# Maxima over the partitions by transposes on TensorE and maxima on VectorE in place of GpSimd's all-reduce, with the opening order of all engines written anew

## The chip, the cores and the metric

The kernel runs on one core of one Trainium2 chip, as one launch. The metric is the device time of an execution in microseconds. In the text PE is TensorE, DVE is VectorE, ACT is ScalarE, GpSimd is also POOL, and SP is SyncE, which here issues all the DMAs.

## The reference

A block of cross-attention and a feed-forward network with quantised weights and activations, over x of 8 x 1024 x 512 and a context of 8 x 64 x 384, all float32:

1. x is normalised (mean and variance over the 512, no weights) and gives q = norm(x) Wq. The context gives k = ctx Wk and v = ctx Wv. There are 8 heads of 64. Softmax of q k / 8 times v, times Wo, plus bo, is added to x.
2. The sum is normalised again and goes through three "bit-linear" layers: silu(norm(x) times w_gate) times (norm(x) times w_up), then w_down (512 x 2048 each), and the result is added to x. Each of these weights is divided by the mean of its absolute values, rounded and clipped to -1, 0, 1. Each row of activations is scaled by 127 over its largest absolute value and rounded.

## The kernel before, in words

**Tiles and stages.** x is cut into 64 tiles of 128 rows, 8 tiles to each of the 8 batches. Attention runs six tiles ahead of the feed-forward part (L = 6). Per tile: stats and rstd (mean, variance and 1/sqrt; the last on GpSimd), x_norm (DVE), x_hi and x_lo (the tile as two float16 halves; ACT and GpSimd), turn_x (a DMA transpose), scores (PE), s_max, expo, e_sum, p_norm, p_hi and p_lo (softmax, and again two halves), turn_p, attend, add_x. Then stats, x_scale, quant_x, copy_x, turn_q (quantise and transpose), gate_up (PE), silu (ACT), mult and h_part (DVE), h_max, quant_h, copy_h, turn_h, down (PE), final and store_y.

**Keys and values are folded into the weights.** For each batch scores multiply by Wq times K (round_X 0 to 3, lines 1067 to 1071) and attend by V times Wo (round_X 4 to 7). K and V lie on block diagonals (block_diag, line 813). All these operands are two float16 halves (hi on ACT, lo on DVE), and so that the halves are exact enough each operand is first scaled by a power of two taken from its largest absolute value.

**The maxima.** Four such values are needed over a whole operand, all partitions included: of Wq (m = 0) and Wo (m = 1), one number each, and of K and V, eight numbers each, one per batch. DVE takes the maximum along each partition (max_w, line 752; max_c, line 758) into mxw; then GpSimd's partition_all_reduce takes it over the partitions and leaves the result on all of them in mxa (lines 532 to 538):

```python
def all_max_w(m):
    eng.wait_ge(v_mw, m + 1)
    eng.partition_all_reduce(mxa[:, m, 0:1], mxw[:, m, 0:1], P, RABS).then_inc(g_mw, 1)
```

scale_w, scale_c and scales (lines 767 to 797) make the powers of two from mxa. What needs them: q_hi, q_lo and o_wide (Wq and Wo in halves), block_diag, and hi and lo.

**The opening.** Setup 0 to 2 transpose the context, setup 3 to 6 make K, 7 to 10 transpose Wq, 11 to 14 make V (line 1025). The three weights of the feed-forward part, 4 MB each, are loaded in four pieces; abs_sum (ACT and DVE) sums their absolute values, total (PE) adds over the partitions, mean (DVE, line 836) gives the scale. Then the pieces are made ternary: 24 quarters through a PE transpose (flip), ACT (tern_flip, line 650) and DVE (clip_flip), the rest through tern, clip and a DMA transpose (turn_w). load_down overwrites gate's pieces and waits for them (line 482). The first gate_up needs all of gate and up.

**What sets the order.** Every engine executes its pieces in the order written and waits by semaphores. Each piece has a due time (put), and the pieces are sorted by it; but those named in the engine's list in OPENING (line 331) come first, in the order of the list. The lists of before reach to about the first tile of the feed-forward part (down 0 on PE). SP's list holds the loads and the DMA transposes, so a turn_x that waits holds back the loads behind it.

## Time and profile before

| what | us |
|---|---|
| median of 3 runs | 1204.06 |
| lowest and highest run | 1202.31, 1204.07 |
| span of the profiled execution | 1203.5 |
| busy in it: PE | 1102.5 |
| busy: DVE | 1091.2 |
| busy: ACT | 701.0 |
| busy: POOL | 429.4 |

The profiled execution has no other time of its own than its span, from the first to the last instruction; the median of the runs is 0.56 us above it. An engine's line in the page shows its busy share in 40 slices of 30 us, in tenths. "Idle before" an instruction is put down to what it waited for last ("<-"); "issue" is idle time for which the trace shows no event.

### The profile page before, as it was taken

The page shows a single profiled execution, that of the slowest core. Times are in us where ns is not written, and L with a number is a line of the kernel's source. Part 1 is how long each engine was busy: PE and PEld are TensorE (multiplying, and loading weights), DVE is VectorE, ACT ScalarE, POOL GpSimd, SP SyncE. Part 2 cuts the span into 40 slices and gives each one's busy share as a digit, 9 for nine tenths or more (in the row PEclk, how much of TensorE's full clock was granted, in tenths as well). Part 3 has the DMA queues.
Part 4 walks back from the last instruction along what each step waited for, and adds up shares of the span by engine and source line. Part 5 has one row for each costly group of instructions (what it writes and reads, how often), then busy time and mean ns, then how long its engine had stood idle before and what let it go on. Part 6 is the DMA issues. An engine that isn't in the chain of part 4 may idle for free.

```text
span 1203.5 us, 17256 instructions
## 1 busy us (share of the span) xinstructions
PE 1102.5 (92%) x5204; PEld 509.8 (42%) x5266; DVE 1091.2 (91%) x2463; ACT 701.0 (58%) x883; POOL 429.4 (36%) x534
## 2 busy tenths in 40 slices
PE   5636889999999999999999999999999999999998
PEld 3323434444444444444444444444444444444433
DVE  4449999999999999999999999999999999999996
ACT  2336676656665665666656665656556665565544
POOL 1037623434343343334333433333333344334100
PEclk9768999999999999999999999999999999999999
DMA  7724585454453454544544555345545455444343
GB/s 279 218 71 114 120 157 101 101 93 99 108 112 85 103 105 110 97 88 105 109 96 93 103 110 106 89 94 110 107 88 104 101 114 105 97 106 81 79 92 92
DMA packets 343484, 130.65 MB, mean 109 GB/s; under 512 B 319968, under 2 KB 320480, under 8 KB 342880
## 3 DMA queue, kind: packets, MB, share of 16 engines
q1 hardware_dynamic: 343392, 129.55, 48.8%
q8 instruction: 42, 0.69, 0.2%
q14 instruction: 50, 0.41, 0.1%
HBM read 34.08 MB, written 16.78 MB: 42 GB/s over the span
## 4 chain that ended last, share of the span: by engine, by line
DVE 48%; PE 27%; issue 15%; DMA 4%; ACT 3%; POOL 1%; DVEq 0%; SPq 0%; ACTq 0%; POOLq 0%
PE ps L1142 13%; DVE FF L882 7%; DVE hm L886 7%; PE ps L1158 5%; DVE bns L868 4%; DVE FF L939 3%; PE ps L1082 3%; PE ps L1083 3%; PE ps L1085 3%; DVE am L940 2%; DVE den L927 2%; DMA FF<-FF 2%; DVE xr L959 2%; DVE xr L874 2%; ACT FF L666 2%
## 5 line engine op out<-in xcount | busy, mean ns | idle before, releaser
L1142 PE MATMUL ps<-wgT,FF 128*128 128x512 bf16 x1024 | 267.7, 384 | 32.3 <-DMA FF<-FF 32.1
L1142 PE MATMUL ps<-wW,FF 128*128 128x512 bf16 x1024 | 267.8, 385 | 0.0
L675 ACT ACTIVATE FF<-FF,c 128x1024 int16<-128x1024 f32 x128 | 140.0, 1141 | 178.6 <-DVE c L896 178.6
L1158 PE MATMUL ps<-wW,FF 128*128 128x512 bf16 x962 | 218.4, 379 | 5.9 <-DMA FF<-FF 2.6
L666 ACT ACTIVATE FF<-ps,sg 128x512 f32<-128x512 f32 x256 | 172.3, 675 | 20.0 <-PE ps L1142 19.2
L886 DVE TENSOR_REDUCE hm<-FF 128x1 f32<-128x512 f32 x256 | 174.2, 680 | 4.6
L882 DVE TENSOR_TENSOR FF<-FF,ps 128x512 f32<-128x512 f32 x256 | 172.3, 673 | 3.1 <-PE ps L1142 2.3
L1142 PEld LDWEIGHTS ps<-wgT,FF 128*128 128x128 bf16 x1024 | 96.5, 98 | 157.9 <-DMA FF<-FF 50.9
L544 POOL TENSOR_SCALAR ve<-mv 128x1 f32<-128x1 f32 x128 | 47.7, 373 | 306.2 <-DVE mv L869 275.5
L1142 PEld LDWEIGHTS ps<-wW,FF 128*128 128x128 bf16 x1024 | 101.2, 99 | 124.9 <-issue 6.6
L1158 PEld LDWEIGHTS ps<-wW,FF 128*128 128x128 bf16 x1024 | 99.9, 98 | 124.3 <-issue 4.5
L564 POOL TENSOR_TENSOR AT<-AT,rd 128x512 f32<-128x512 f32 x64 | 66.9, 1045 | 230.8 <-DVE rd L931 230.8
L682 ACT ACTIVATE xhl<-xn 128x512 f16<-128x512 f32 x64 | 40.3, 629 | 146.7 <-DVE xn L910 145.1
L552 POOL TENSOR_TENSOR xhl<-xn,xhl 128x512 f16<-128x512 f32 x64 | 74.6, 1166 | 109.5 <-ACT xhl L682 102.8
L1082 PE MATMUL ps<-MV,xT 128*128 128x512 f16 x256 | 99.4, 388 | 4.7 <-DVE AT L921 4.2
L1083 PE MATMUL ps<-MV,xT 128*128 128x512 f16 x256 | 99.3, 388 | 0.0
L1082 PE MATMUL ps<-MV,pT 128*128 128x512 f16 x256 | 97.0, 379 | 0.6 <-DVE MV L809 0.6
L1083 PE MATMUL ps<-MV,pT 128*128 128x512 f16 x256 | 97.0, 379 | 0.0
L693 ACT ACTIVATE AT<-AT 128x512 f16<-128x512 f32 x64 | 40.3, 630 | 90.5 <-POOL AT L564 86.5
L572 POOL TENSOR_TENSOR AT<-AT 128x512 f16<-128x512 f32 x64 | 74.1, 1158 | 51.9 <-POOL AT L564 44.5
L546 POOL TENSOR_TENSOR rs<-ve,half 128x1 f32<-128x1 f32 x128 | 84.6, 661 | 10.7
L868 DVE BATCH_NORM_STATS2 bns<-xr 128x6 f32<-128x512 f32 x128 | 86.1, 673 | 0.5 <-DMA xr<-in_x 0.5
(120 smaller groups left out, 1647.3 us busy)
## 6 DMA issues: line engine op xcount, KB each, us to landing
xr<-in_x SPq DMA_DIRECT2D x64, 256.0 KB, 2.8
out<-xr SPq DMA_DIRECT2D x64, 256.0 KB, 2.0
FF<-in_L_ffn_w_gate SPq DMA_DIRECT2D x4, 1024.0 KB, 11.7
wW<-in_L_ffn_w_up SPq DMA_DIRECT2D x4, 1024.0 KB, 8.9
FF<-in_L_ffn_w_down SPq DMA_DIRECT2D x4, 1024.0 KB, 5.3
FF<-FF SPq DMA_TRANSPOSE x192, 3.2
MV<-in_L_xattn_Wq SPq DMA_DIRECT2D x1, 1024.0 KB, 8.2
MV<-in_L_xattn_Wo SPq DMA_DIRECT2D x1, 1024.0 KB, 11.8
```

The costliest lines, as they stand in the source:

```text
L546: eng.tensor_tensor(rs[:, t:t + 1], ve[:, t:t + 1], half[:, :], ALU.pow).then_inc(end, 1)
L552: eng.tensor_tensor(xhl[:, 1, :], xn[:, :], xhl[:, 0, :], ALU.subtract).then_inc(g_xl, 1)
L572: eng.tensor_tensor(phl[:, 1, :], E[:, j % 2, :], phl[:, 0, :], ALU.subtract).then_inc(g_pl, 1)
L666: eng.activation(h[:, i % 2, f * 512:(f + 1) * 512], G[n % 2][:, :], ACT.Silu, scale=sg[:, i:i + 1]).then_inc(a_si, 1)
L675: eng.activation(q16h[:, 1024 * z:1024 * z + 1024], h[:, t % 2, 1024 * z:1024 * z + 1024], ACT.Copy, scale=c2[:, t:t + 1]).then_inc(a_qh, 1)
L868: link(eng.bn_stats(bns[:, k, t % 2, :], xr[:, t % R, :]))
L882: eng.tensor_tensor(hh, hh, U[n % 2][:, :], ALU.mult).then_inc(v_h, 1)
L886: ins = eng.tensor_reduce(hm[:, f:f + 1], h[:, i % 2, f * 512:(f + 1) * 512], AX_X, ALU.max, apply_absolute_value=True)
L1082: eng.matmul(bank[:, :], T[:, k, :], hi[:, k, :], start=(k == 0), stop=False)
L1083: eng.matmul(bank[:, :], T[:, k, :], lo[:, k, :], start=False, stop=False)
L1142: mm = eng.matmul(bank[n % 2][:, :].rearrange("p (o f) -> p o f", o=4), qxT[:, i % 2, k, :], w[:, 4 * f:4 * f + 4, k, :], start=(k == 0), ...
L1158: mm = eng.matmul(y_bank(i)[:, :], hT[:, i % 2, c, :], wdT[:, c, :], start=(c == 0), stop=(c == 15))
```

## The change

The four partition_all_reduce calls and their semaphores go. Each of the four maxima (e = 0 and 1: Wq and K; e = 2 and 3: Wo and V) now takes five steps on PE and DVE: max_turn transposes a 128 x 128 tile whose first columns hold the maxima of the partitions (PE, into a PSUM bank); max_fold takes the maximum along each row of it and copies that over 128 columns (DVE); max_spread transposes this back, so that each partition has all the numbers (PE); max_take copies them into mxa (DVE). The tile mxc is cleared by GpSimd at the start. e = 0 uses the bank of scores, the others that of attend. round_X 0 and 1 and attend 0 get waits for these banks.

The lists of all five engines in OPENING are written anew and are longer: SP's to load_x 14, PE's to gate_up 5 2, DVE's to copy_h 4 1. In SP's list x 0 comes before Wq, gate 3 and the loads of up before turn_x 0, gate 2 after gate 3. In DVE's list stats 1 to 3 and block_diag 1 0 come earlier, before mean 0. The diff, with each list cut to its beginning:

```diff
 def xattn_ffn(nc, x, ctx_768, Wq, Wk, Wv, Wo, bo, w_gate, w_up, w_down, out):
@@ -120,7 +119,9 @@
         wsum = sb("wsum", [P, 3, 4], F32)
         wst = sb("wst", [P, 3, 4], F32)
         mxq = sb("mxq", [P, 2, 4, NB], F32)
-        mxw = sb("mxw", [P, 2, 1 + NB], F32)
+        mxc = sb("mxc", [P, 4, P], F32)
+        mxr = sb("mxr", [P, P], F32)
+        mxf = sb("mxf", [P, 4], F32)
         mxa = sb("mxa", [P, 2, 1 + NB], F32)
         e2 = sb("e2", [P, 2, NB], F32)
         inv = sb("inv", [P, 2, NB], F32)
@@ -162,10 +163,13 @@
         v_mx = sem("v_mx")
         g_ow = sem("g_ow")
         v_mw = sem("v_mw")
-        g_mx = sem("g_mx")
+        g_mc = sem("g_mc")
+        p_mt = sem("p_mt")
+        v_mf = sem("v_mf")
+        p_mb = sem("p_mb")
+        v_mc = sem("v_mc")
         v_ch = sem("v_ch")
         v_sc = sem("v_sc")
-        g_mw = sem("g_mw")
         v_sw = sem("v_sw")
         v_sk = sem("v_sk")
         a_wh = sem("a_wh")
@@ -328,66 +332,93 @@
         def bank_of(n):
             return FIRST_BANKS[n] if n < 8 else pX
 
+
+        def max_bank(e):
+            return pS if e == 0 else pA
+
+        def max_dst(e):
+            m = e // 2
+            return mxa[:, m, 0:1] if e % 2 == 0 else mxa[:, m, 1:1 + NB]
+
             "sync": (
+                "load_ctx, load_wk, load_x 0, load_wq, load_x 2, load_x 3, load_gate 0, load_x 8, load_bo, load_up "
+                "0, load_wv, load_gate 1, load_x 1, load_wo, load_gate 3, load_up 1, load_gate 2, load_up 2, load_x "
+                "7, turn_x 0, load_up 3, load_x 5, load_x 4, load_x 6, turn_x 1, load_down 0, turn_x 2, load_down "
+                "1, turn_x 3, turn_p 0, load_down 2, turn_x 4, turn_p 1, load_down 3, turn_p 2, turn_x 5, turn_p 3, "
...
             "gpsimd": (
+                "constants, rstd 0 0, x_lo 0, add_bo 0, rstd 1 0, rstd 2 0, rstd 3 0, add_bo 1, o_wide 0, o_wide 1, "
+                "o_lo 0, o_lo 1, o_wide 2, o_wide 3, x_lo 1, o_lo 2, o_lo 3, add_bo 2, x_lo 2, add_bo 3, p_norm 0, "
+                "x_lo 3, p_lo 0, rstd 4 0, p_norm 1, add_bo 4, x_lo 4, p_lo 1, rstd 5 0, add_bo 5, rstd 6 0, rstd 7 "
...
             "scalar": (
+                "evac 0, evac 2, x_hi 0, evac 4, evac 5, evac 6, q_hi 0, q_hi 1, q_hi 2, q_hi 3, evac 11, abs_sum 0 "
+                "1, evac 12, evac 13, hi 0 0, hi 0 1, hi 0 2, abs_sum 0 3, abs_sum 1 0, abs_sum 1 1, evac 14, hi 0 "
+                "3, o_hi 0, o_hi 1, x_hi 1, o_hi 2, o_hi 3, abs_sum 1 3, tern_flip 0 0 0, tern_flip 0 0 1, "
+                "tern_flip 0 0 2, tern_flip 0 0 3, x_hi 2, tern_flip 0 1 0, tern_flip 0 1 1, expo 0, tern_flip 0 1 "
...
             "vector": (
+                "evac 1, stats 0 0, x_norm 0, max_w 0, evac 3, max_c 0 0, max_fold 0, max_c 0 1, abs_sum 0 0, "
+                "max_take 0, max_c 0 2, scale_w 0, max_c 0 3, q_lo 0, max_fold 1, q_lo 1, max_take 1, q_lo 2, "
+                "scale_c 0, q_lo 3, block_diag 0 0, scales 0, stats 1 0, stats 2 0, stats 3 0, x_norm 1, max_w 1, "
+                "max_c 1 1, lo 0 0, lo 0 1, lo 0 2, block_diag 1 0, max_fold 2, max_c 1 2, max_take 2, max_c 1 0, "
+                "scale_w 1, abs_sum 0 2, max_c 1 3, mean 0, max_fold 3, abs_sum 1 2, lo 0 3, max_take 3, scale_c 1, "
+                "block_diag 0 1, x_norm 2, clip_flip 0 0 0, clip_flip 0 0 1, s_max 0, clip_flip 0 0 2, clip_flip 0 "
+                "0 3, clip_flip 0 1 0, clip_flip 0 1 1, x_norm 3, scales 1, e_sum 0, clip_flip 0 1 2, s_max 1, "
+                "clip_flip 0 1 3, stats 4 0, clip_flip 0 2 0, e_sum 1, s_max 2, x_norm 4, clip_flip 0 2 1, "
...
             "tensor": (
+                "setup 0, setup 1, setup 2, setup 3, setup 4, max_turn 0, setup 5, max_spread 0, setup 6, setup 7, "
+                "setup 8, setup 9, setup 10, max_turn 1, max_spread 1, setup 11, setup 12, setup 13, round_X 0 0, "
+                "round_X 0 1, round_X 0 2, round_X 0 3, setup 14, max_turn 2, max_spread 2, total 0, max_turn 3, "
+                "max_spread 3, flip 0 0 0, flip 0 0 1, scores 0, total 1, flip 0 0 2, flip 0 0 3, round_X 0 4, flip "
...
         block = ctx.enter_context(nc.Block())
@@ -528,14 +559,7 @@
                 eng.memset(kbd[:, :, :, :], 0.0).then_inc(g_c, 1)
                 eng.memset(vbd[:, :, :, :], 0.0).then_inc(g_c, 1)
                 eng.wait_ge(g_c, 4)
-
-            def all_max_w(m):
-                eng.wait_ge(v_mw, m + 1)
-                eng.partition_all_reduce(mxa[:, m, 0:1], mxw[:, m, 0:1], P, RABS).then_inc(g_mw, 1)
-
-            def all_max(m):
-                eng.wait_ge(v_mx, m + 1)
-                eng.partition_all_reduce(mxa[:, m, 1:1 + NB], mxw[:, m, 1:1 + NB], P, RABS).then_inc(g_mx, 1)
+                eng.memset(mxc[:, :, :], 0.0).then_inc(g_mc, 1)
 
                 mv, ve, rs, done, mid, end = ((mv1, ve1, rs1, v_st1, g_ve1, g_rs1),
@@ -584,10 +608,6 @@
             for c in range(4):
                 put(25.9 + c, o_wide, c)
                 put(26.1 + c, o_lo, c)
-            put(MAXW_T[0] + 2.3, all_max_w, 0)
-            put(MAXW_T[1] + 2.3, all_max_w, 1)
-            put(MAX_T[0], all_max, 0)
-            put(MAX_T[1], all_max, 1)
             for s in range(FIRST, LAST + 1):
                 if 0 <= j + 1 < NT:
@@ -752,7 +772,8 @@
             def max_w(m):
                 eng.wait_ge((l_wq, l_wo)[m], 16)
                 src = (wq_sb, wo_sb)[m]
-                eng.tensor_reduce(mxw[:, m, 0:1], src.rearrange("p c n -> p (c n)"), AX_X, ALU.max,
+                eng.wait_ge(g_mc, 1)
+                eng.tensor_reduce(mxc[:, 2 * m, 0:1], src.rearrange("p c n -> p (c n)"), AX_X, ALU.max,
                                   apply_absolute_value=True).then_inc(v_mw, 1)
 
             def max_c(m, q):
@@ -761,11 +782,23 @@
                                         ALU.max, apply_absolute_value=True)
                 link(ins)
                 if q == 3:
-                    eng.tensor_reduce(mxw[:, m, 1:1 + NB], mxq[:, m, :, :].rearrange("p q b -> p b q"), AX_X,
+                    eng.wait_ge(g_mc, 1)
+                    eng.tensor_reduce(mxc[:, 2 * m + 1, 0:NB], mxq[:, m, :, :].rearrange("p q b -> p b q"), AX_X,
                                       ALU.max).then_inc(v_mx, 1)
 
+            def max_fold(e):
+                eng.wait_ge(p_mt, e + 1)
+                if e >= 1:
+                    eng.wait_ge(p_mb, e)
+                link(eng.tensor_reduce(mxf[:, e:e + 1], max_bank(e)[:, 0:P], AX_X, ALU.max))
+                eng.tensor_copy(mxr[:, :], mxf[:, e:e + 1].to_broadcast([P, P])).then_inc(v_mf, 1)
+
+            def max_take(e):
+                eng.wait_ge(p_mb, e + 1)
+                eng.tensor_copy(max_dst(e), max_bank(e)[:, 0:1 if e % 2 == 0 else NB]).then_inc(v_mc, 1)
+
             def scale_w(m):
-                eng.wait_ge(g_mw, m + 1)
+                eng.wait_ge(v_mc, 2 * m + 1)
                 link(eng.tensor_scalar(we[:, m, 0:1].bitcast(I32), mxa[:, m, 0:1].bitcast(I32), 0x7F800000, None,
                                        ALU.bitwise_and))
                 link(eng.tensor_scalar(we[:, m, 0:1], we[:, m, 0:1], 2.0 ** -45, 2.0 ** 45, ALU.max, ALU.min))
@@ -773,7 +806,7 @@
                 eng.tensor_scalar(wf[:, m:m + 1], we[:, m, 1:2], 2.0 ** 14, None, ALU.mult).then_inc(v_sw, 1)
 
             def scale_c(m):
-                eng.wait_ge(g_mx, m + 1)
+                eng.wait_ge(v_mc, 2 * m + 2)
                 link(eng.tensor_reduce(ke[:, m, 0:1], mxa[:, m, 1:1 + NB], AX_X, ALU.max))
                 link(eng.tensor_scalar(ke[:, m, 1:2].bitcast(I32), ke[:, m, 0:1].bitcast(I32), 0x7F800000, None,
                                        ALU.bitwise_and))
@@ -785,7 +818,7 @@
                 back = (2.0 ** -11, 2.0 ** -23)[m]
                 eng.wait_ge(v_sk, m + 1)
                 eng.wait_ge(v_sw, m + 1)
-                eng.wait_ge(g_mw, m + 1)
+                eng.wait_ge(v_mc, 2 * m + 2)
                 link(eng.tensor_scalar(e2[:, m, :], mxa[:, m, 1:1 + NB], mxa[:, m, 0:1], None, ALU.mult))
                 link(eng.tensor_scalar(e2[:, m, :].bitcast(I32), e2[:, m, :].bitcast(I32), 0x7F800000, None,
                                        ALU.bitwise_and))
@@ -968,6 +1001,9 @@
                 put(MAXW_T[m], max_w, m)
                 for q in range(4):
                     put(SET_E[(3, 11)[m] + q] + .7, max_c, m, q)
+                for e, w in ((2 * m, (MAXW_T[0] + 1, MAX_T[0] + 3)[m]), (2 * m + 1, MAX_T[m])):
+                    put(w + .6, max_fold, e)
+                    put(w + .9, max_take, e)
                 put(MAXW_T[m] + 3.2, scale_w, m)
                 put(MAX_T[m] + 1.2, scale_c, m)
                 put(MAX_T[m] + 1.3, block_diag, 0, m)
@@ -1049,9 +1085,24 @@
                                         start=(a == 0), stop=(a == 2))
                 mm.then_inc(p_set, 1)
 
+            def max_turn(e):
+                eng.wait_ge((v_mw, v_mx)[e % 2], e // 2 + 1)
+                if e == 0:
+                    eng.wait_ge(g_id, 2)
+                elif e >= 2:
+                    eng.wait_ge(v_lo, 2)
+                    eng.wait_ge(v_mc, e)
+                eng.transpose(max_bank(e)[:, 0:P], mxc[:, e, :], ident[:, :]).then_inc(p_mt, 1)
+
+            def max_spread(e):
+                eng.wait_ge(v_mf, e + 1)
+                eng.transpose(max_bank(e)[:, 0:P], mxr[:, :], ident[:, :]).then_inc(p_mb, 1)
+
             def round_X(b, r):
                 n = 8 * b + r
                 bank = bank_of(n)
+                if n < 2:
+                    eng.wait_ge(v_mc, n + 1)
                 if r < 4:
                     eng.wait_ge(v_kb, 4 * b + 4)
                 else:
@@ -1099,6 +1150,8 @@
                 eng.wait_ge(t_p[j % 2], 16 * (j // 2 + 1))
                 if j % TPB == 0:
                     eng.wait_ge(v_lo, 8 * b + 8)
+                if j == 0:
+                    eng.wait_ge(v_mc, 4)
                 if j >= 1:
                     eng.wait_ge(v_x1, j)
                 three(pA, pT[:, j % 2, :, :], part(b, 2), part(b, 3)).then_inc(p_A, 1)
@@ -1160,6 +1213,9 @@
 
             for r in range(SETUP):
                 put(SET_T[r], setup, r)
+            for e, w in enumerate((MAXW_T[0] + 1, MAX_T[0], MAX_T[0] + 3, MAX_T[1])):
+                put(w + .5, max_turn, e)
+                put(w + .8, max_spread, e)
             for r in range(8):
                 put(RND_T[r], round_X, 0, r)
             for m in range(3):
```

## Rows read from the trace of the kernel before

**Rows 1.** The page, section 1, and the slices of DVE in section 2.
```profile
PE 1102.5 (92%) x5204; PEld 509.8 (42%) x5266; DVE 1091.2 (91%) x2463; ACT 701.0 (58%) x883; POOL 429.4 (36%) x534
...
DVE  4449999999999999999999999999999999999996
```
**Rows 2.** DVE by stretch: stretch, length, busy, instructions; PEclk, DMA share, GB/s.
```profile
0.00:50.00 50.00, 23.94 (x44) 0.83 0.68 236
50.00:100.00 50.00, 23.20 (x45) 0.70 0.34 106
...
200.00:1186.00 986.00, 941.65 (x2152) 0.99 0.48 100
```
**Rows 3.** Who DVE waited for, whole run: us in total, times, longest.
```profile
DVE xn L910 <- POOL rs L546: 23.7, 3, 9.6
DVE ke L777 <- POOL mxa L538: 8.8, 2, 7.3
DVE MV L809 <- ACT MV L632: 7.7, 14, 1.6
DVE xr L750 <- PE ps L1035: 7.2, 1, 7.2
DVE we L769 <- POOL mxa L534: 5.9, 1, 5.9
...
DVE mxw L755 <- DMA MV<-in_L_xattn_Wq: 2.1, 1, 2.1
```
**Rows 4.** Timeline of the opening: start, us, engine, instruction, idle before.
```profile
14.49 0.41 POOL L534 PARTITION_ALL_REDUCE mxa<-mxw  x1 [10.83 <-issue]
...
17.54 0.18 DVE L869 BATCH_NORM_AGGREGATE mv<-bns 128x2 f32<-128x6 f32 x1
...
25.24 0.25 POOL L544 TENSOR_SCALAR ve<-mv 128x1 f32<-128x1 f32 x1 [10.35 <-issue]
...
40.65 0.39 POOL L538 PARTITION_ALL_REDUCE mxa<-mxw  x1 [9.86 <-issue]
...
92.23 1.38 DVE L910 TENSOR_SCALAR xn<-xr,mv,rs 128x512 f32<-128x512 f32 x1 [7.24 <-POOL rs L546]
```
**Rows 5.** Groups of DVE by shape, 0 to 160 us.
```profile
L809 DVE SCALAR_TENSOR_TENSOR MV<-ps,fwd,MV 128x512 f16<-128x512 f32 x11 | 8.1, 740 | 1.3 <-ACT MV L632 1.2
...
L755 DVE TENSOR_REDUCE mxw<-MV 128x1 f32<-128x2048 f32 x2 | 4.6, 2282 | 2.1 <-DMA MV<-in_L_xattn_Wq 2.1
...
L760 DVE TENSOR_REDUCE mxq<-kT 128x8 f32<-128x512 f32 x4 | 2.7, 674 | 0.4 <-ACT kT L611 0.4
...
L777 DVE TENSOR_REDUCE ke<-mxa 128x1 f32<-128x8 f32 x2 | 0.3, 161 | 8.8 <-POOL mxa L538 8.8
```
**Rows 6.** Timeline of PE, transposes and V projection.
```profile
28.02 1.12 PE L1040 MATMUL ps<-ident,MV 128*128 128x128 f32 x4 [5.43 <-ACT kT L611]
...
45.65 5.11 PE L1048 MATMUL ps<-xr,MV 128*128 128x512 f32 x6
...
51.26 2.79 PE L1048 MATMUL ps<-xr,MV 128*128 128x512 f32 x6
```
**Rows 7.** DMA of the first 60 us, in 40 slices of 1.5 us.
```profile
GB/s 0 126 392 380 385 401 377 396 318 399 401 391 384 385 391 381 86 0 0 0 180 135 324 356 399 404 396 78 0 0 5 0 0 115 115 279 355 393 411 378
DMA packets 9526, 14.88 MB, mean 248 GB/s; under 512 B 2401, under 2 KB 2913, under 8 KB 9524
```
**Rows 8.** Landmark lines: duration ns min/median/max, first and last start.
```profile
L841 DVE TENSOR_SCALAR wst<-wst x3: 154/154/155, 68.5 to 135.7; 128x1 f32<-128x1 f32 x3
...
L656 ACT ACTIVATE FF<-ps,wst x24: 664/679/687, 74.3 to 144.5; 128x512 int16<-128x512 f32 x24
...
L1142 PE MATMUL ps<-wgT,FF x1024: 379/379/634, 153.4 to 1187.4; 128*128 128x512 bf16 x171
```
**Rows 9.** Copy_x and x_norm, the same view.
```profile
L954 DVE CAST FF<-FF x64: 283/852/1149, 142.4 to 1177.3; 128x512 bf16<-128x512 int16 x64
...
L910 DVE TENSOR_SCALAR xn<-xr,mv,rs x64: 535/538/1377, 26.3 to 1101.4; 128x512 f32<-128x512 f32 x64
```

More of the change, by code:

```diff
@@ L25 @@
 I32 = mybir.dt.int32
-RABS = bass.bass_isa.ReduceOp.absmax
 def xattn_ffn(nc, x, ctx_768, Wq, Wk, Wv, Wo, bo, w_gate, w_up, w_down, out):
@@ L329, in bank_of @@
             return FIRST_BANKS[n] if n < 8 else pX
+        def max_bank(e):
[3 more added lines that the diff above has]
+            return mxa[:, m, 0:1] if e % 2 == 0 else mxa[:, m, 1:1 + NB]
         OPENING = {
             "sync": (
-                "load_ctx, load_wk, load_wq, load_gate 0, load_gate 1, load_x 0, load_gate 2, load_x 1, load_wv, "
-                "load_x 2, load_wo, turn_x 0, load_gate 3, load_up 0, load_up 1, turn_x 1, load_up 2, load_x 3, "
-                "load_up 3, load_bo, load_x 4, load_x 5, turn_x 2, load_down 0, load_x 6, load_x 7, load_down 1, "
[4 rows of a table removed]
-            "gpsimd": (
[6 rows of a table removed]
-            "scalar": (
[13 rows of a table removed]
-            "vector": (
[18 rows of a table removed]
-            "tensor": (
-                "setup 0, setup 1, setup 2, setup 3, setup 4, setup 5, setup 6, setup 7, setup 8, setup 9, setup "
[9 rows of a table removed]
+                "load_ctx, load_wk, load_x 0, load_wq, load_x 2, load_x 3, load_gate 0, load_x 8, load_bo, load_up "
+                "0, load_wv, load_gate 1, load_x 1, load_wo, load_gate 3, load_up 1, load_gate 2, load_up 2, load_x "
[7 rows of a table added]
+            "gpsimd": (
[8 rows of a table added]
+            "scalar": (
[16 rows of a table added]
+            "vector": (
[26 rows of a table added]
+            "tensor": (
[14 rows of a table added]
         }
```

100 rows, old and new, of the table OPENING are left out of this document.

## The prediction

> **What bounds the kernel now.** I read the page first, then DVE's busy time by stretch, then who DVE waited for, then the timeline of GpSimd in the opening. The reader is to see in the first [rows 1] that DVE and PE are both over 90% busy and that the missing part lies in the first four slices of 30 us: DVE shows 4, 4, 4 there, then 9 to the end. By stretch [rows 2] DVE is busy 23.94 of the first 50 us and 23.20 of the second 50, so it idles 52.9 us in 100; from 200 to 1186 us it is busy 941.65 of 986 (95.5%), and the rest is mostly the short gaps between linked small instructions. DVE is in order and full after the opening, so the end moves by what DVE loses or gains in the opening.
>
> Who ended those idle times [rows 3]: the wait of x_norm for GpSimd's rs 23.7 us in 3 times, ke for mxa 8.8 in 2, we for mxa 5.9 in 1. That is 38.4 us. The other waits are small: 7.2 until the first transposes of ctx are done, 7.7 in 14 times for hi on ACT, 2.1 for Wq.
>
> Why GpSimd was late [rows 4]: an all-reduce itself lasts 0.4 us, but the instruction after the first one starts 10.35 us behind its end, though its input (stats 0 on DVE) was there at 17.7; the second all-reduce has 9.86 idle us before it. The two others repeat this. So each change between ordinary work and the all-reduce, in either direction, costs GpSimd up to ten us in which it does nothing, and all that is behind it in its order waits too: rstd, x_lo (and by it turn_x and the loads behind turn_x in SP's queue), o_wide, add_bo.
>
> **The Trainium skill** on this. Its page GPSIMD Engine Reference, section 4.1 (Engine selection), names GpSimd for a reduction along the partitions, which speaks against the change; and section 2.1 (Instruction dispatch) has some 6 us for the first call of a freshly loaded kernel. By that price, as an estimate, four calls would be worth 24 us, and the sum below would give 1186. The trace disagrees in size: it shows idle time on both sides of the call and up to 10.35 us, and the measurement decides.
>
> **What is removed.** All four all-reduces, and with them the 38.4 us of DVE's waits. x_norm still waits for rstd, but rstd is then two short instructions, the first of 0.25 us [rows 4]; I take 0.9 for both with their hand-over.
>
> **What is added on DVE.** Per maximum: a reduce of 128x128 out of PSUM, a copy spread to 128x128, and a copy of one to eight columns. No row has these sizes. From below a reduce to 128x1 of 8 columns takes 0.16, from above one of 512 columns takes 0.68 [rows 5]. By length between them 120/504 of the way: 0.28. I take 0.28 for the reduce, the same for the copy, and 0.18 for the last: 0.74, four times 3.0 us. Floor 4 x 0.48 = 1.9, ceiling 4 x 1.56 = 6.2; nothing here can be a gain, since DVE had no part in it before.
>
> **What is added on PE**, two transposes of 128x128 each, eight in all. Four such transposes take 1.12 us at the lower clock [rows 6], 0.28 each: 2.2 us. They stand in a stretch in which PE idled for GpSimd anyway, so they cost nothing by themselves. The waits they add do count. max_spread stands in PE's queue behind a fold on DVE. With e=0 setup 6 is behind it: PE does setup 5 meanwhile (2.6 us), the fold needs 0.6. With e=1 setup 11 is behind it, which waits for q_lo 1 in any case. With e=2 and 3 total 0 and the flips are behind it. On DVE the take stands behind max_c and abs_sum (e=0), q_lo (e=1), max_c (e=2), abs_sum and lo (e=3), each 0.68 us or more, against a hop over PE of about 0.5. If all this cover were gone: eight hops, 4 us. The clearing of mxc falls where GpSimd was idle from 3.7 to 14.5 [rows 4]; it costs nothing. The waits of round_X 0, 1 and attend 0 for the takes hold nothing, since block_diag or the setup is later.
>
> **What moves.** Loads: x 0 goes ahead of Wq, so Wq lands later by 256 KB; at the 380 to 400 GB/s of the DMA row [rows 7] that is 0.7 us, and stats 0 and x_norm 0 now fill the time. gate 3 stood behind turn_x 0, which hung on GpSimd; now all of gate and three pieces of up stand ahead of it, and turn_x 0 itself no longer waits long. The last of gate (gate 2) has 12.3 MB up to its end in the queue (3 x 768, 8 x 1024, 6 x 256 KB), 31.5 us at 0.39 MB per us, so it lands near 33.5; abs_sum 0 2 comes up on DVE at about 44. It is hidden by 10 us. At the mean rate of the same view, 248 GB/s, it would land at 51.5 and cost 8.
>
> DVE up to the end of mean 0 (the point from which weights can be made ternary): the new list has 36.4 us of work ahead of it, of which max_c 8 x 0.674, max_w and abs_sum (the same shape) 4 x 2.28 and q_lo and lo 7 x 0.74 make 19.7 [rows 5], and evac, stats, scale, block_diag, scales, fold and take 16.7 by the smaller groups of the same view. To it come 7.2 until the first evac and the waits: 0.9 for rstd 0, 0.4 for Wq, 0.4 for setup 3, 1.2 for max_turn 0 (it follows setup 4), 0.8 for the last K evac, 3.7 in all. So mean 0 ends at 47.3, against 68.7 [rows 8]: 21.4 earlier, and with 5.0 us more DVE work done (block_diag 1 0, three max_c, lo 0 2, stats 3, less x_norm 2). Behind it the last all-reduce's two waits are gone, 1.5 for ke (8.8 less the longer one, 7.3 [rows 3]) and 7.2 for x_norm at 92.2 [rows 4], 8.7 in all, less 0.7 for fold 3: 8.0. Together 34.4.
>
> Does PE keep up with this? K is done as early as now, and block_diag 0 ends near 29, no longer behind an all-reduce. Setup 11 to 13 need 3 x 2.79 us at the full clock [rows 6] and run from 25 to 33; round_X and hi 0 0 follow by 34, and lo 0 0 comes up on DVE at 37. ACT has the tern_flips, 24 x 0.68 = 16.3 [rows 8], and ran them over 70 us; it has room.
>
> **The sum.** By waits: 38.4 removed, less 3.0 added work, less new waits. In the sparse part these (3.7) take the place of the present small ones (2.1 and three of 0.5 or less), so nearly nothing; in the dense part from 47 us on, all engines now run closer and I allow 3.5, six or so waits of the size of those of lo for hi (7.7 us in 14) [rows 3]. 38.4 - 3.0 - 3.5 = 31.9. By the landmark: 34.4 less the same allowance, 30.9. I take 32. Profiled execution: 1203.5 - 32 = 1171.5. The median of the runs, 1204.06, lies 0.56 above that span; so 1172.
>
> The steady part I leave as it is: its order is not rewritten and GpSimd follows DVE in it.
>
> **Rivals.**
> 1. Other waits take half of the place. If PE falls to the lower clock level after the transposes, setup 11 to 13 take 3 x 5.11 instead of 3 x 2.79 [rows 6], 7.0 more, and hi 0 0 comes at 41 instead of 34: lo 0 0 on DVE waits 4. For it: the six passes at 45.65 ran at the lower level (5.11), behind an idle PE. Against: PE idles little before it in the new order. With it come ACT waits, another 14 x 0.55 = 7.7, where tern_flip, hi and exp now crowd: 32 - 4 - 7.7 = 20.3, 1184.
> 2. The loads run at the mean 248 GB/s: 8 of the gain is lost, 1180. Against: where there is enough in the queue the row stays at 380 to 400.
> 3. More is won: the new lists reach tile 5 and also remove the wait for Wq and a third of those for hi (2.1 and 2.6 [rows 3]), and the allowance is not needed: 38.4 - 3.0 + 4.7 = 40.1, 1164.
> 4. Slower. DVE's copy_x, which has GpSimd's p_norm beside it in the steady part, takes 0.85 us in the median and 0.28 at the least; x_norm takes 0.54 in the median but up to 1.38 [rows 9]. If the new opening left the engines in another phase, so that x_norm too met GpSimd in every tile, it would cost 0.84 x 54 tiles = 45 us against the 32 won: 1217. It decides from 0.6 us per tile on. Against: GpSimd starts p_norm on DVE's own e_sum, so the phase is set by DVE's order, which is the same.
> 5. No change: DVE's waits just pass to PE or the loads whole. The landmarks leave no room for it.
>
> **How the numbers follow.** Forecast 0.69 (its own range 1166 to 1179), rival 1 0.17, rival 2 0.03, rival 3 0.07, rival 4 0.03, rival 5 0.01. Range: added work up to 6.2, hops uncovered 4 and rival 1 at 1184 above, rival 3 at 1164 below: 1163 to 1186. Faster by over 0.2% (2.4 us, about what a measurement of this kernel can tell from no change) 0.96, within it 0.01, slower 0.03.
>
> **What would show it.** Right: no wait of DVE for GpSimd over 2 us in the first 100; the first tern_flip near 50 instead of 74.3; the first gate_up near 121 to 124 instead of 153.4 [rows 8]; DVE busy some 37 to 40 in each of the first two 50 us; DVE's total busy time 3 us up; copy_x and x_norm per tile unchanged. Wrong: a wait of DVE for PE at max_fold over 2 us, setup 11 to 13 at 5.1 us each, abs_sum waiting for gate, or the first gate_up early but the last tile's end not.

## The result, and the profile after

The median fell from 1203.71 us (four runs, 1202.31 to 1204.07) to **1172.42 us** (four runs, 1170.53 to 1173.20): ratio 0.9747, 95% interval 0.9732 to 0.9762. The forecast was 1172.0. The profiled execution took 1171.69, its span is 1169.9 against 1203.5, 33.6 less. One of the four runs of e5 fell into a slower state (1442.96 us at a granted clock of 0.75 in place of 0.98) and is left out of e5's numbers. The page after, to be held against [rows 1]:

```profile
PE 1102.5 (94%) x5274; PEld 508.3 (43%) x5274; DVE 1086.9 (93%) x2475; ACT 698.0 (60%) x881; POOL 415.4 (36%) x531
...
DVE  5998997899999999999999999999999999999996
```
DVE's first four slices, 4, 4, 4, 9 before, are now 5, 9, 9, 8. DVE's stretches (stretch, length, busy, PEclk, DMA share, GB/s), against [rows 2]:

```profile
0.00:50.00 50.00, 37.49 (x79) 0.94 0.92 315
50.00:100.00 50.00, 43.29 (x104) 0.89 0.54 137
```
That is 33.6 us more work done by 100 us (80.8 against 47.1), as much as the span lost: the gain was made in the first 100 us. What came behind cancels: DVE's work in all is 4.3 us less (1091.2 to 1086.9), and behind 100 us it idles 4.3 us more. Who DVE waited for in the whole run (total, times, longest), against [rows 3]:

```profile
DVE MV L842 <- ACT MV L652: 9.3, 14, 2.3
DVE xr L770 <- PE ps L1071: 7.3, 1, 7.3
DVE xr L992 <- PE ps L1136: 6.4, 3, 2.9
...
DVE mxf L793 <- PE ps L1095: 1.3, 1, 1.3
...
DVE xn L943 <- POOL rs L570: 1.0, 1, 1.0
...
DVE mxc L776 <- DMA MV<-in_L_xattn_Wq: 0.2, 1, 0.2
```
GpSimd's 38.4 us are down to 1.0. The new maxima, in the timeline (start, length, instruction, idle before), on DVE and on PE, with the transposes' neighbours:

```profile
16.49 0.29 DVE L793 TENSOR_REDUCE mxf<-ps 128x1 f32<-128x128 f32 x1 [1.28 <-PE ps L1095]
16.82 0.73 DVE L794 COPY mxr<-mxf 128x128 f32<-128x128 f32 x1
20.39 0.15 DVE L798 COPY mxa<-ps 128x1 f32<-128x1 f32 x1
24.13 0.23 DVE L794 COPY mxr<-mxf 128x128 f32<-128x128 f32 x1
...
24.42 0.33 PE L1099 MATMUL ps<-ident,mxr 128*128 128x128 f32 x1 [0.79 <-DVE mxr L794]
25.23 7.96 PE L1084 MATMUL ps<-xr,MV 128*128 128x512 f32 x18 [0.48 <-DVE wqT L835]
```
The landmarks (shortest, median, longest ns, first and last start), against [rows 8, 9]:

```profile
L874 DVE TENSOR_SCALAR wst<-wst x3: 153/154/154, 46.2 to 87.9; 128x1 f32<-128x1 f32 x3
...
L676 ACT ACTIVATE FF<-ps,wst x24: 667/681/702, 53.7 to 105.7; 128x512 int16<-128x512 f32 x24
...
L1195 PE MATMUL ps<-wgT,FF x1024: 376/379/634, 113.6 to 1153.8; 128*128 128x512 bf16 x171
...
L987 DVE CAST FF<-FF x64: 271/853/856, 105.4 to 1143.7; 128x512 bf16<-128x512 int16 x64
...
L943 DVE TENSOR_SCALAR xn<-xr,mv,rs x64: 533/538/1243, 9.9 to 1067.4; 128x512 f32<-128x512 f32 x64
```

### The profile page after: what moved, and what is told of

Its sections match the earlier page's. It is cut to its first block, busy times and chain, and to the rows that moved or that the text cites. A ratio compares the mean times of both kernels' runs of the same rounds, so it can differ in the third digit from the quotient of the medians.

```text
span 1169.9 us, 17337 instructions
## 1 busy us (share of the span) xinstructions
PE 1102.5 (94%) x5274; PEld 508.3 (43%) x5274; DVE 1086.9 (93%) x2475; ACT 698.0 (60%) x881; POOL 415.4 (36%) x531
## 4 chain that ended last, share of the span: by engine, by line
DVE 50%; PE 16%; issue 12%; ACT 4%; DMA 2%; POOL 1%; DVEq 0%; ACTq 0%; POOLq 0%
DVE FF L915 9%; DVE hm L919 8%; PE ps L1195 7%; DVE bns L901 4%; DVE FF L972 3%; DVE am L973 3%; PE ps L1211 3%; DVE den L960 2%; DVE xr L907 2%; DVE xr L992 2%; ACT FF L686 2%; DVE MV L842 2%; DMA FF<-FF 2%; PE ps L1133 2%; DVE FF L937 2%
## 5 line engine op out<-in xcount | busy, mean ns | idle before, releaser
L1195 PE MATMUL ps<-wgT,FF 128*128 128x512 bf16 x1024 | 265.6, 382 | 28.1 <-DMA FF<-FF 25.9
L1195 PE MATMUL ps<-wW,FF 128*128 128x512 bf16 x1024 | 267.3, 384 | 0.9 <-DVE FF L915 0.9
L1211 PE MATMUL ps<-wW,FF 128*128 128x512 bf16 x1024 | 231.3, 379 | 2.7 <-DMA FF<-FF 2.7
L686 ACT ACTIVATE FF<-ps,sg 128x512 f32<-128x512 f32 x256 | 172.6, 676 | 22.7 <-PE ps L1195 21.8
L568 POOL TENSOR_SCALAR ve<-mv 128x1 f32<-128x1 f32 x128 | 32.4, 253 | 295.7 <-DVE mv L902 295.6
L1133 PE MATMUL ps<-MV,pT 128*128 128x512 f16 x256 | 98.6, 385 | 6.8 <-DMA pT<-AT 5.8
L1134 PE MATMUL ps<-MV,pT 128*128 128x512 f16 x256 | 98.5, 385 | 0.0
L582 POOL TENSOR_TENSOR xr<-xr,bo_sb 128x512 f32<-128x512 f32 x64 | 82.2, 1285 | 18.6 <-DVE xn L943 14.8
## 6 DMA issues: line engine op xcount, KB each, us to landing
MV<-in_L_xattn_Wo SPq DMA_DIRECT2D x1, 1024.0 KB, 12.7
```

The costliest lines, as they stand in the source:

```text
L582: eng.tensor_tensor(xr[:, t % R, :], xr[:, t % R, :], bo_sb[:, :], ALU.add).then_inc(g_xb, 1)
L686: eng.activation(h[:, i % 2, f * 512:(f + 1) * 512], G[n % 2][:, :], ACT.Silu, scale=sg[:, i:i + 1]).then_inc(a_si, 1)
L1133: eng.matmul(bank[:, :], T[:, k, :], hi[:, k, :], start=(k == 0), stop=False)
L1134: eng.matmul(bank[:, :], T[:, k, :], lo[:, k, :], start=False, stop=False)
L1195: mm = eng.matmul(bank[n % 2][:, :].rearrange("p (o f) -> p o f", o=4), qxT[:, i % 2, k, :], w[:, 4 * f:4 * f + 4, k, :], start=(k == 0), ...
L1211: mm = eng.matmul(y_bank(i)[:, :], hT[:, i % 2, c, :], wdT[:, c, :], start=(c == 0), stop=(c == 15))
```

## The experiments

Ratios are to the kernel before, run beside each on the same chip; "the changed kernel" is the one of the change (0.9747).

### The exchange and the order, each alone

**e1**: the changed maxima in the old lists (evac 3, stats 0, lo 0 1 and x_norm 2 moved ahead of scale_w, so that DVE has work while PE transposes).

```
-"... abs_sum 0 0, scale_w 0, evac 3, stats 0 0, max_c 0 0 ..."   (vector)   gpsimd: without all_max_w, all_max
+"... abs_sum 0 0, evac 3, max_fold 0, stats 0 0, max_take 0, scale_w 0, max_c 0 0 ..."
+"... lo 0 1, max_fold 2, x_norm 2, max_take 2, scale_w 1 ..."   (folds and takes 1 and 3 only put in)
+"setup 4, max_turn 0, setup 5, max_spread 0 ..."   (tensor)
```


> Only the exchange: the four maxima by transposes and folds, in the old lists of all five engines, with max_turn, max_fold, max_spread and max_take put in where the all-reduces' results were used. Theory (GpSimd's idle time around the all-reduces was the cost): 38.4 us of DVE's waits go, 3 us of work come, and since the old order isn't fitted to it some 6 to 8 us of waits for PE, ACT and the loads take their place: about 1176 to 1180, and DVE shows no wait for GpSimd over 2 us. Rival (the rewritten order is what gains): the larger part of the gain is missing, 1190 or more.

Measured: 1175.27, ratio 0.9774 [0.9757, 0.9791], just below the range of the theory. DVE's waits:

```profile
DVE MV L825 <- ACT MV L635: 10.2, 15, 1.7
...
DVE mxf L776 <- PE ps L1078: 7.4, 3, 5.2
```
The exchange alone brings nearly all, and no wait for GpSimd is left that the profile shows. In the old order the folds wait 7.4 us for their transposes where the new lists leave 1.3, and at 100 us DVE has done 74.8 us of work against 80.8. Yet the order's part in the time is only some 3 us (1175.27 against 1172.42, the intervals just overlap), and DVE's waits sum to 41.4 here and 41.7 in the changed kernel. The new lists lose most of their lead right behind their end. DVE's list ends with copy_h 4 1, at 193.0 us; behind it stand, in the changed kernel:

```profile
196.73 0.75 DVE L842 SCALAR_TENSOR_TENSOR MV<-ps,fwd,MV 128x512 f16<-128x512 f32 x1 [1.66 <-ACT MV L652]
199.83 0.75 DVE L842 SCALAR_TENSOR_TENSOR MV<-ps,fwd,MV 128x512 f16<-128x512 f32 x1 [2.34 <-ACT MV L652]
```
With five more waits up to 211.7 us it is 9.2 us between 130 and 250 us, against 1.1 in e1 and 3.0 in the kernel before; e3, with the new lists, has 10.8 there. No run has a smoother passage from the list to the due times; what it would bring is open.

**e2**: the old all-reduces in the new lists, at four places in GpSimd's list: three stand ahead of idle times that GpSimd has in the changed kernel (3.9, 13.9 and 7.6 us), the last where it is busy.

```
-max_turn, max_spread, max_fold, max_take (all lists)
+gpsimd: "... x_lo 0, all_max_w 0, add_bo 0, all_max 0, ... add_bo 1, all_max_w 1, ... o_wide 3, all_max 1 ..."
```


> Only the order: the new lists, but with the four all-reduces, which stand in GpSimd's list behind x_lo 0, add_bo 0, add_bo 1 and o_wide 3. Theory: each all-reduce blocks GpSimd for 15 to 20 us, about 72 in all, of which some 21 fall on GpSimd's idle time in the changed kernel (13.9 before rstd 1, 7.6 before o_wide 0); rstd 1 to 3 and DVE behind them wait: 1205 to 1225, no faster than before. Rival (the order gains by itself): 1190 or less.

Measured: 1205.65, ratio 1.0020 [1.0008, 1.0033]. DVE's waits, and its second stretch:

```profile
DVE ke L795 <- POOL mxa L556: 25.8, 2, 14.5
...
DVE xn L928 <- POOL xhl L570: 5.5, 1, 5.5
```
```profile
50.00:100.00 50.00, 26.59 (x58) 0.66 0.23 69
```
With the all-reduces at these places the order by itself wins nothing: 36.0 us of waits for GpSimd remain (25.8, 5.5, 2.9 for rs and 1.8 for we), at other instructions. Other places for them were not tried.

### What an all-reduce costs

**e3**: the changed kernel with four all-reduces whose result nobody reads; in e4 and e5 only one of them.

```
+def spare(e):
+    eng.wait_ge((v_mw, v_mx)[e % 2], e // 2 + 1)
+    eng.partition_all_reduce(mxd[:, e, 0:w], mxc[:, e, 0:w], P, RABS)
+gpsimd: spare 0 behind x_lo 0, 1 behind add_bo 0, 2 behind add_bo 1, 3 behind o_wide 3
```


> The changed kernel with four all-reduces more at those same places in GpSimd's list, whose results nobody reads; the exchange gives the maxima. Theory: what costs is that GpSimd stands still, not that DVE waits for a maximum; most of the loss comes back, 1195 to 1215, and the waits are those of x_norm for rs. Rival (DVE's wait for the result is the cost): 1172 to 1176.

Measured: 1205.42, ratio 1.0030 [1.0018, 1.0042], as slow as before. DVE's waits, and GpSimd's timeline:

```profile
DVE xn L954 <- POOL xhl L585: 20.2, 1, 20.2
DVE xn L954 <- POOL rs L579: 13.8, 2, 12.8
```
```profile
20.79 0.41 POOL L571 PARTITION_ALL_REDUCE mxd<-mxc  x1 [8.18 <-issue]
28.52 1.42 POOL L591 TENSOR_TENSOR xr<-xr,bo_sb 128x512 f32<-128x512 f32 x1 [7.33 <-issue]
...
77.56 0.39 POOL L571 PARTITION_ALL_REDUCE mxd<-mxc  x1 [5.88 <-issue]
85.42 1.14 POOL L585 TENSOR_TENSOR xhl<-xn,xhl 128x512 f16<-128x512 f32 x1 [7.47 <-issue]
```
Nobody waits for the results, and still DVE waits 34.0 us (1.0 in the changed kernel): for rs and xhl, which GpSimd makes afterwards. The cost is not the reduction (0.4 us) nor its latency, but the idle time on both sides of it: 8.2 and 7.3, 6.2 and 8.9, 5.9 and 7.3, 5.9 and 7.5 us, 57 in all, of which DVE feels 33. The Trainium skill, page GPSIMD Engine Reference, section 2.1 (Instruction dispatch), has one such pause of some 6 us for the first call of a newly loaded kernel. The idle time ahead of the second to fourth call, 5.9 to 6.2 us, is of that size; the 7.3 to 8.9 us behind the calls are not in it, and the pauses come at each of the four calls, not at the first only. What GpSimd does in them no trace here shows.

**e4**, spare 3 alone, where all engines are busy:

> The changed kernel with one unused all-reduce, behind o_wide 3, where GpSimd is busy. Theory: x_lo 1 and o_lo behind it start 15 to 20 us later and DVE meets this at s_max 0 or lo 0 4: plus 6 to 15 us, 1178 to 1187. Rival: 1172.

Measured: 1180.40, ratio 0.9819 [0.9799, 0.9840]. **e5**, spare 1 alone, where GpSimd has nothing to do from 17.5 to 31.3 us:

> The changed kernel with one unused all-reduce where GpSimd idles: behind add_bo 0 (17.5 us) and before rstd 1 (31.3 us), on the maxima of K, which are there at 23.2. Theory: an all-reduce costs only by the time in which GpSimd stands still and has something to do; the step into it falls on 17.5 to 24, the step back (7 to 9 us) ends at 32 to 33, so x_norm 1 is held 1 to 2 us: 1172 to 1175. Rival (the all-reduce disturbs other engines or the DMAs by itself): 1180 as with the one in the dense stretch.

Measured: 1172.22 in the median of three runs (1171.10 to 1175.02), ratio 0.9746 [0.9712, 0.9780]. GpSimd in both, first e4, then e5:

```profile
55.07 0.39 POOL L571 PARTITION_ALL_REDUCE mxd<-mxc  x1 [5.69 <-issue]
62.38 1.14 POOL L585 TENSOR_TENSOR xhl<-xn,xhl 128x512 f16<-128x512 f32 x1 [6.92 <-issue]
```
```profile
25.08 0.39 POOL L571 PARTITION_ALL_REDUCE mxd<-mxc  x1 [7.40 <-issue]
33.71 0.25 POOL L577 TENSOR_SCALAR ve<-mv 128x1 f32<-128x1 f32 x1 [8.24 <-DVE mv L913]
```
The same call costs 8 us in one place and nothing that shows in the other. In e4, x_norm waits 12.7 us for xhl, yet the time rises by 8: DVE's other waits are 2.3 us shorter, and its busy time is 2.2 less. In e5 most of the standstill runs down while GpSimd would have waited anyway: the call starts 1.5 us after its input is there (23.6 us), and rstd 1 2.1 us after stats 1 (31.6 us).

### Is the opening bound by DVE's work alone

**e6** gives DVE four more maxima of 128x2048 in the opening, behind clip_flip 0 0 3, 0 2 0, 0 3 2 and 1 0 0; **e8** gives PE the scores of tiles 1 to 4 twice (the first sums are overwritten).

```
+def extra(n):                       # e6, n in 0 to 3, placed by DVE's list
+    eng.tensor_reduce(mxd[:, n:n + 1], kT as 128x2048, AX_X, ALU.max, apply_absolute_value=True)
+if 1 <= j <= 4:                     # e8, in scores(j)
+    three(pS, xT[:, j % 2, :, :], part(b, 0), part(b, 1))
```


> The changed kernel with four more reduces of 128x2048 on DVE (2.29 us each, 9.2 in all, result unused), spread over the ternary stretch of the opening (behind clip_flip 0 0 3, 0 2 0, 0 3 2 and 1 0 0). Theory (DVE in order sets the end, the account was by DVE): plus 8 to 9.2 us, 1180 to 1182. Rival (PE or the chain through ACT and the transposes bounds the opening): plus 0 to 4, 1172 to 1176.

Measured: 1180.45, ratio 0.9820 [0.9784, 0.9856].

> The changed kernel in which PE does the twelve matmuls of scores twice for tiles 1 to 4, in the same stretch: 48 matmuls of 0.216 us, 10.4 us more on PE and 2.6 us later scores each time. Theory (DVE bounds, PE has slack there): plus 1 to 6 us, 1173 to 1178. Rival (PE bounds as much): plus 10, 1182.

Measured: 1177.58, ratio 0.9789 [0.9760, 0.9818]; DVE's waits for the scores:

```profile
DVE mx L950 <- PE ps L1136: 7.4, 8, 2.8
```
In the changed kernel this wait is 2.3 us in 6 times. 9.2 us of DVE's work cost 8, 10.4 of PE's cost 5: behind DVE, PE is near too.

**e7** fills three waits with work that was ready: stats 1 before fold 0 (x 1 loaded before x 2), clip_flip 1 0 2 and x_scale 1 before add_x 2.

```
-"max_c 0 0, max_fold 0 ..." "add_x 2, clip_flip 1 0 2, x_scale 1 ..." "load_x 2, load_x 3 ... load_x 1"
+"max_c 0 0, stats 1 0, max_fold 0 ..." "clip_flip 1 0 2, x_scale 1, add_x 2 ..." "load_x 1, load_x 3 ... load_x 2"
```


> The changed kernel with two waits of DVE filled: stats 1 stands before max_fold 0, which waited 1.3 us (x 1 is loaded in the place of x 2), and clip_flip 1 0 2 and x_scale 1 stand before add_x 2, which waited 2.9 us. Theory (each us of DVE's waits in the opening is a us of the end): minus 2 to 3.5, 1169 to 1170. Rival (another wait takes the place at once): 1172.

Measured: 1172.54, ratio 0.9743 [0.9717, 0.9770]: a miss. The fold waits 0.4 us in place of 1.3, and the 2.9 of add_x 2 are gone. By 100 us DVE has done 1.1 us more work (81.9 against 80.8), but the end does not come earlier. These waits grew (0.8 and 0.0 before the edit; the second is x_scale 1's):

```profile
DVE kT L771 <- PE ps L1085: 1.2, 1, 1.2
DVE FF L973 <- ACT FF L720: 1.1, 1, 1.1
```
The rival held: other waits took the place of those filled. By what path the microsecond is lost behind 100 us isn't shown.

### The clash of DVE and GpSimd in the steady part

Rival 4 rested on copy_x taking 0.85 us beside p_norm and 0.28 in clear [rows 9]. x_scale's subtraction (L972) does the same: 0.47 to 0.48 in clear, 0.86 in the median beside add_bo. Both clashes are in both kernels. One due time each takes them out (between 200 and 1140 us copy_x in every tile, x_scale in 46 of 57):

```
-return at(t - 1, (.1, .12, .5,   .62, .7,   .72)[n])
+return at(t - 1, (.1, .12, .5,   .62, .715, .72)[n])   # e9: copy_x later
+return at(t - 1, (.1, .12, .515, .62, .715, .72)[n])   # e10: both later
+return at(t - 1, (.1, .12, .515, .62, .7,   .72)[n])   # e12: x_scale later
```


> The changed kernel with one due time of DVE's copy_x moved from .700 to .715 of a tile, so that it stands behind h_part 2 (which reads PSUM) in every tile of the steady part and no longer runs beside GpSimd's p_norm. The opening lists are the same. It asks whether the clash that rival 4 of the prediction priced is a cost in both kernels. Theory (DVE sets the steady part, and a cast beside GpSimd takes 0.80 us in the mean instead of 0.28 in clear): copy_x falls to about 0.3, some 0.5 us for each of 57 tiles, 28 us of DVE time; TensorE has about 50 us idle in the stretch, so most of it shows, and the time is 1146 to 1156, with copy_x below 0.4 us. Rival (TensorE, or the round trip that a tile's transposes make over the DMA queue, sets the steady part): copy_x gets shorter all the same, but DVE waits longer for TensorE or TensorE for the loads, and the time stays at 1168 to 1174, or rises because quantised x is sent later. Second rival: copy_x merely meets another operation of GpSimd and stays near 0.8; 1170 to 1175.

Measured: 1171.97, ratio 0.9744 [0.9728, 0.9760]: my theory missed, the first rival held. First one tile of the changed kernel in the timeline, then one of e9:

```profile
705.22 1.04 POOL L588 TENSOR_TENSOR AT<-AT,rd 128x512 f32<-128x512 f32 x1 [3.72 <-DVE rd L964]
...
705.55 0.86 DVE L987 CAST FF<-FF 128x512 bf16<-128x512 int16 x1
```
```profile
706.53 1.04 POOL L588 TENSOR_TENSOR AT<-AT,rd 128x512 f32<-128x512 f32 x1 [3.72 <-DVE rd L964]
...
707.59 0.28 DVE L987 CAST FF<-FF 128x512 bf16<-128x512 int16 x1
...
707.61 0.63 ACT L713 ACTIVATE AT<-AT 128x512 f16<-128x512 f32 x1 [1.46 <-POOL AT L588]
708.14 0.67 ACT L686 ACTIVATE FF<-ps,sg 128x512 f32<-128x512 f32 x1
...
708.85 0.69 DVE L915 TENSOR_TENSOR FF<-FF,ps 128x512 f32<-128x512 f32 x1 [0.32 <-ACT FF L686]
```
The first cast ends at 706.41, 0.15 behind the end of p_norm (706.26), and it does so in all 52 tiles of this stretch in which it starts beside p_norm; x_scale's subtraction ends 0.28 to 0.29 behind add_bo in 45. The Trainium skill, page SBUF — State Buffer, section "SBUF: two separate sides", has a reason: a DVE operation in a two-port mode and a GpSimd operation share a port pair under an exclusive lock, the first holds it for its whole length, and the other is blocked. Its section "Who interferes with whom" counts casts and tensor_scalar among the operations that can be in such a mode. The traces agree, here and for x_scale. In e9 the cast is free (0.28). But it now stands one place later on DVE, and so the quantised x is ready no earlier: in the tile shown copy_x ends 5.65 us after the start of x_scale (707.87 - 702.22), against 5.50 in the changed kernel (706.41 - 700.91), and gate_up starts 8.13 us after it against 7.98. DVE doesn't gain either: ACT's silu stands in its queue behind p_hi, and p_hi waits for that same p_norm; so DVE reaches h_part before silu is done and waits: 14.0 us in 43 times over the run, against 0.9 in one. The chain from rd over p_norm, p_hi and silu to h_part keeps its length whatever DVE does meanwhile.

> As the kernel with copy_x later, and x_scale too is moved from .500 to .515 of a tile, behind h_part 1, so that its subtraction of 128x512 (0.84 us in the mean, 0.47 in clear) no longer runs beside GpSimd's add_bo. Theory (DVE sets the steady part): another 0.37 x 57 = 21 us of DVE time; TensorE then is the nearer bound, so half or more of it shows: 1135 to 1148. Rival (TensorE or the round trip over the DMA queue sets it): no more than 2 us below the kernel with copy_x later alone, or slower than it, since x_scale and the quantisation behind it on ACT start later. If copy_x alone already brings nothing, this brings nothing either: 1168 to 1176.

Measured: 1152.75, ratio 0.9592 [0.9566, 0.9617]: between the theory's range and the rival's, 19 us below e9. So x_scale counts where copy_x did not, and one more run is to say whether it needs copy_x.

> The changed kernel with DVE's x_scale alone moved from .500 to .515 of a tile; copy_x stays beside GpSimd's p_norm. With copy_x alone moved the time had not changed (1171.97), with both moved it fell to 1152.75. Theory A (x_scale stands at the head of the chain that sends a tile's quantised x to TensorE: x_scale, ACT's quantisation, copy_x, the transposing load, gate_up; a gain at its head counts, one of copy_x was eaten by the wait for silu behind it): x_scale alone brings most of it, 1152 to 1158, and TensorE's wait for the loads falls from 26 to about 17 us. Theory B (DVE time only shows once both casts are short): 1164 to 1171. Rival: moving x_scale alone brings copy_x in a worse place: 1172 or more.

Measured: **1149.73**, ratio 0.9558 [0.9537, 0.9580], the lowest median of all: x_scale alone does it, below even the range of theory A (PE's wait for the loads, forecast near 17 us, is 15.8). Its two casts over 200 to 1140 us (busy, mean ns), then copy_x's landmark line:

```profile
L972 DVE TENSOR_SCALAR FF<-xr,mv 128x512 f32<-128x512 f32 x57 | 29.6, 519 | 0.1
...
L987 DVE CAST FF<-FF 128x512 bf16<-128x512 int16 x57 | 45.8, 804 | 0.6 <-ACT FF L719 0.2
```
```profile
L987 DVE CAST FF<-FF x64: 273/853/856, 105.5 to 1122.3; 128x512 bf16<-128x512 int16 x64
```
and in the same stretch PE's longest wait, first in the changed kernel, then in e12:

```profile
PE ps L1195 <- DMA FF<-FF: 25.9, 19, 2.2
```
```profile
PE ps L1195 <- DMA FF<-FF: 15.8, 12, 1.7
```
From the first copy_x to the last a tile takes 16.48 us in the changed kernel ((1143.7 - 105.4) / 63), 16.49 in e9 (106.3 to 1144.9), 16.14 in e12: 0.34 less, 21.4 us in all, where x_scale lost 0.32 (0.843 to 0.519). That the two are nearly alike doesn't mean that each tile gains what x_scale lost: the tiles gain unevenly (0.1 to 1.7 us), and TensorE's clock has a part. Between 300 and 914 us PE waits in every fourth tile some 2 us for the transposed x, which x_scale begins. Such a wait in the changed kernel and what followed it, then the same tile in e12:

```profile
435.64 1.36 PE L1195 MATMUL ps<-wgT,FF 128*128 128x512 bf16 x4 [2.16 <-DMA FF<-FF]
436.80 1.91 PE L1195 MATMUL ps<-wW,FF 128*128 128x512 bf16 x4
```
```profile
432.74 1.04 PE L1195 MATMUL ps<-wgT,FF 128*128 128x512 bf16 x4 [1.47 <-DMA FF<-FF]
```
Behind five of the ten long waits (1.9 to 2.2 us) of the changed kernel the granted clock is 0.50 for some 3 us (the lower level, 1.2 GHz; it was 1.00 ahead of them), and each of these five tiles takes 1.3 us more than its like (17.6 against 16.3). In e12 the ten waits are 1.5 to 1.7 us, in e10 1.6 to 1.9, and the clock stays at 1.00 behind all of them; in e9 they are 2.0 to 2.2, and it falls behind five. So of e12's 21.4 us some 10 are less waiting of PE (25.9 to 15.8), some 6 are the lower clock that no longer follows (5 x 1.3, an estimate), and 5 I can't assign. The chain from x_scale's start to gate_up is 7.98 us in the tile shown for the changed kernel, 8.13 in e9 and 6.99 in e12 (699.11 - 692.12). That this chain, rather than DVE's sum, makes the difference between the two casts fits all these runs; another cause in the tile's order isn't excluded by them.

**e11** is e10 with the three fills of e7.

> The kernel with both pieces moved, together with the three fills of waits in the opening (stats 1 before fold 0, tile 1 loaded before tile 2, clip_flip 1 0 2 and x_scale 1 before add_x 2), which by themselves had brought nothing. If TensorE's and ACT's chains set the opening, as that run suggests, nothing again: 1151 to 1154. If the fills only lacked a faster steady part: 1149 to 1151.

Measured: 1150.90, ratio 0.9571 [0.9545, 0.9597]; e10, e11 and e12 can't be told apart by their intervals. So no gain of the fills or of copy_x's move over the one moved due time of e12 can be seen; 1150.90 lies at the edge of both ranges expected, and whether the fills bring 1 or 2 us over e10 is open.

## Why the prediction was right, step by step

- **The sum.** It had 38.4 of removed waits, less 3.0 of added work, less 3.5 of new waits, 31.9. The traces have 37.4 (38.4 less the remaining 1.0), DVE's busy time 4.3 *less* (1091.2 to 1086.9), and new waits of 8.4: all of DVE's waits sum to 70.7 before and 41.7 after, 29.0 less, where 37.4 went. 37.4 + 4.3 - 8.4 = 33.3 of the span's 33.6. So the total was met with two terms off by 5 and 7 us in opposite directions; the mechanism was right, and part of the closeness is luck.
- **Span and median.** I had taken the median as 0.56 above the span of the profile. In each of the four runs after, the time is 1.8 us above the span. If that holds before too, the profiled execution before took some 1205.3 us (an estimate), 1.6 above its median. So the spans fell by 33.6 and the medians by 31.3, against 32 forecast for both; that 1172.0 met 1172.42 is luck in this as well.
- **The removed waits**: right, and e3 shows that they were GpSimd's standstill. Of the 9.86 us that I read ahead of the second all-reduce 1.2 were a wait for its input (there at 32.0 us); the other 8.6 stand.
- **The added work**: three instructions of 0.29, 0.23 to 0.73 and 0.15 us, forecast 0.28, 0.28, 0.18. They sum to 3.6 (forecast 3.0; two of the four copies, at 0.73 and 0.60, made the difference). **"DVE's total busy time 3 us up" failed**: what fell is the time of casts and tensor_scalars: the second set of the six 128x8 tensor_scalars of scales 6.5 to 2.2 us, wgT's casts 8.1 to 6.0, copy_x 50.4 to 48.4, x_norm 36.4 to 35.3. As I read it they met GpSimd's work less often, by the clash shown below e9. The two long copies are the two that have GpSimd beside them.
- **The new waits**: this is the term that was mis-sized: 3.5 allowed, 8.4 measured, net of the 1.9 won at Wq. New are fold 1.3, kT 0.8, 1.6 more for hi on ACT, and 6.4 at L992, which I had not named. It was also misplaced. I allowed it for the dense part of the opening; but up to 130 us DVE's waits fell by 35.2 (51.3 to 16.1), and 6.2 of the 8.4 came between 130 and 250 us (3.0 to 9.2), where the new lists end (see e1). The longest, 2.9 at 98.4 us, has this on PE ahead of it:

```profile
93.06 0.61 PE L1133 MATMUL ps<-MV,pT 128*128 128x512 f16 x1 [3.62 <-DMA pT<-AT]
```
PE stood 3.6 us and then went at the lower clock (granted 0.50 from 93 to 97 us, 0.61 to 0.63 us per matmul; 0.38 from 98.4 on), which was rival 1's mechanism at a smaller size and 60 us later than where rival 1 had it. V's projections (setup 11 to 13) ran at full clock (granted 1.00 from 22 to 34 us): 18 matmuls in 7.96 us.
- **The landmarks.** mean 0 ended at 46.3, forecast 47.3, right. First tern_flip at 53.7, forecast near 50, late: ACT's queue reached it only then, since o_wide on GpSimd held it and an abs_sum followed:

```profile
49.77 0.63 ACT L640 ACTIVATE wo<-MV 128x512 f16<-128x512 f32 x1 [2.63 <-POOL MV L601]
...
51.85 1.89 ACT L660 ACTIVATE xr<-wW 128x2048 bf16<-128x2048 f32 x1
```
It cost nothing that shows later. First gate_up at 113.6, forecast 121 to 124: 39.8 us earlier, while the last is only 33.6 earlier. The work left for DVE at that point is the same (993.6 us before, 993.0 after), but the stretch behind it is 6.2 us longer: this is the gap where the new lists end. DVE was busy 37.5 and 43.3 us in the first two 50, forecast 37 to 40 in each; no wait for GpSimd was over 1.0 us, as forecast.
- **Steady part unchanged**: right. The medians of copy_x (852 to 853 ns) and x_norm (538) are the same, and rival 4 did not come. But I had priced such a clash at the full time that it holds DVE, and the runs don't bear that out: e9 took 29.6 us of it away (45.5 to 15.9) and nothing moved, and at x_scale's place (e12) 17.6 us of it (47.2 to 29.6) brought 22.7, because PE's waits and its clock hang on it too.
- **Loads**: hidden, as forecast; the wait for Wq is 0.2 us and abs_sum never waited for gate.

## What to carry to other kernels

A custom operation of GpSimd among its ordinary ones costs what GpSimd can't do around it (12.6 to 15.5 us per call in e3 and e4), not what the operation takes; call it where GpSimd is idle, or make the maximum with two transposes and a fold, 0.7 to 1.2 us of DVE. Before spending effort on the order of an opening, try the exchange in the old order: it had nine tenths of the gain. And look for instructions whose median is far above their shortest: if a neighbour on GpSimd holds them, moving the one at the head of the chain behind its next neighbour can be worth much more than a rewritten order (22.7 us here, 1172.42 to 1149.73, against some 3). A hand-written list of an opening must also be looked at where it ends: here DVE waits 6.2 us more at the seam than before.
